# Probability split of a macaron attention layer: the low half moved ahead on VectorE, the high half moved between two exponentials on ScalarE

## The reference

```python
x = x + 0.5 * ffn(layernorm(x))
x = x + attn(layernorm(x), Wq, Wk, Wv, Wo, head_scale)
x = x + 0.5 * ffn(layernorm(x))
# attn: 16 heads of 128 over 4 key/value heads, rotary on q and k, causal
scores = einsum('bhid,bhjd->bhij', q, k) / sqrt(128)
attn = softmax(where(causal, scores, lowest))
out = einsum('bhij,bhjd->bhid', attn, v) * head_scale @ Wo
# ffn: ternary weights, hidden = silu(x wu) * (x wg), then wd
```

## Time and profile before

| | |
|---|---|
| median of 3 runs | 1085.21 us (1085.12 to 1085.38) |
| the profiled execution's own time | 1085.6 us |
| its span | 1083.8 us |
| busy, share of the span | PE 99%, DVE 85%, ACT 75%, POOL 66% |
| TensorE clock granted | 1.00 throughout |
| attention | about 187 to 909 us of the span |

### The profile page before, as it was taken

How to read it: one execution, slowest core, us unless ns; L and a number is a source line. 1 busy time by engine, 2 the same in 40 slices (tenths; PEclk the granted TensorE clock), 3 DMA queues, 4 the chain that set the end, 5 groups by cost and what they waited for, 6 DMA issues and landing times.

```text
span 1083.8 us, 26934 instructions
## 1 busy us (share of the span) xinstructions
PE 1068.4 (99%) x8537; PEld 845.5 (78%) x8537; DVE 921.7 (85%) x2313; ACT 815.3 (75%) x2040; POOL 713.0 (66%) x906
## 2 busy tenths in 40 slices
PE   8999999999999999999999999999999999999998
PEld 6556566788888888888888888888888887565665
DVE  6787886989999999999999999999999996433333
ACT  7887996887778787787877878778788785444443
POOL 3567675776777677777777777777777674444443
PEclk9999999999999999999999999999999999999999
DMA  9623222334434433343343433434334343100101
GB/s 346 169 40 59 52 47 39 52 74 87 74 72 82 80 73 76 71 82 75 73 81 71 82 70 73 82 73 82 71 69 82 73 82 70 30 19 19 39 19 39
DMA packets 262167, 79.94 MB, mean 74 GB/s; under 512 B 249329, under 2 KB 260849, under 8 KB 261873
## 3 DMA queue, kind: packets, MB, share of 16 engines
q1 hardware_dynamic: 261696, 79.19, 35.4%
q10 hardware_dynamic: 432, 0.27, 0.1%
HBM read 12.85 MB, written 4.19 MB: 16 GB/s over the span
## 4 chain that ended last, share of the span: by engine, by line
PE 73%; issue 10%; POOL 6%; ACT 5%; DVE 4%; DMA 1%; POOLq 0%; DVEq 0%; ACTq 0%; SPq 0%
PE bank L770 44%; PE bank L829 14%; POOL SCR L427 6%; PE bank L727 5%; PE bank L739 5%; PE bank L759 5%; ACT SCR L637 2%; DVE ARENA L1155 1%; ACT ARENA L644 1%; DVE SCR L973 1%; DVE bank L1179 1%; DMA SCR<-ARENA 0%; DVE X L963 0%; ACT SCR L515 0%; ACT ARENA L582 0%
## 5 line engine op out<-in xcount | busy, mean ns | idle before, releaser
L452 POOL TENSOR_SCALAR SCR<-SCR,RI 128x128 f32<-128x128 f32 (+1 forms) x512 | 309.5, 604 | 44.3 <-DVE RI L1151 4.2
L637 ACT ACTIVATE SCR<-bank,NM 128x128 f32<-128x128 f32 (+1 forms) x512 | 208.2, 419 | 123.4 <-DVE NM L1179 123.3
L417 POOL TENSOR_TENSOR SCR<-SCR 128x512 f32<-128x512 f32 x160 | 203.2, 1270 | 147.6 <-DVE SCR L973 146.1
L427 POOL TENSOR_TENSOR SCR<-SCR 128x512 f16<-128x512 f32 x128 | 151.0, 1182 | 161.2 <-ACT SCR L515 159.0
L829 PE MATMUL bank<-SCR 128*128 128x128 f32 (+1 forms) x1024 | 193.7, 332 | 4.1 <-ACT SCR L637 3.0
L534 ACT COPY SCR<-bank 64x512 f32<-64x512 f32 x320 | 185.5, 580 | 14.1 <-PE bank L770 8.2
L992 DVE SCALAR_TENSOR_TENSOR SCR<-SCR,CS,bank 128x512 f32<-128x512 f32 x128 | 95.1, 743 | 113.3 <-PE bank L739 100.2
L1155 DVE TENSOR_TENSOR ARENA<-SCR,ARENA 128x768 f16<-128x768 f32 x128 | 187.1, 1462 | 4.5 <-ACT ARENA L644 3.9
L770 PE MATMUL bank<-WOH,ARENA 128*128 128x256 f16 x1024 | 188.3, 273 | 0.8 <-DVE X L1188 0.8
L1179 DVE CUSTOM_DVE_ANT_0 bank<-bank,MASK,SCQ 128x128 f32<-128x128 f32 (+1 forms) x512 | 183.1, 417 | 3.5 <-PE bank L829 2.7
L545 ACT ACTIVATE SCR<-bank,SU 128x512 f32<-128x512 f32 x128 | 87.6, 685 | 106.4 <-PE bank L727 104.8
(11 more groups left out here) (120 smaller groups left out, 1653.1 us busy)
## 6 DMA issues: line engine op xcount, KB each, us to landing
out<-X SPq DMA_DIRECT2D x7, 512.0 KB, 2.9
X<-in_x SPq DMA_DIRECT2D x1, 2560.0 KB, 10.8
ARENA<-in_wq SPq DMA_DIRECT2D x1, 2048.0 KB, 13.8
ARENA<-in_wo SPq DMA_DIRECT2D x1, 2048.0 KB, 18.8
SCR<-ARENA SPq DMA_TRANSPOSE x128, 3.6
X<-in_x SPq DMA_DIRECT2D x3, 512.0 KB, 9.9
X<-in_wu SPq DMA_DIRECT2D x2, 512.0 KB, 5.8
X<-in_wg SPq DMA_DIRECT2D x2, 512.0 KB, 7.4
```

Of the source, the lines that this page charges most:

```text
L417: gp.tensor_tensor(dst, M1[:, m, :], M2[:, m, :], ALU.add).then_inc(add, 1)
L427: gp.tensor_tensor(HL[layer][:, f % 4, :], H32[layer][:, f % 2, :], HH[layer][:, f % 4, :], ALU.subtract).then_inc(s["hl_done"], 1)
L452: last = gp.tensor_scalar(EX[:, par, lo:hi], EX[:, par, lo:hi], RI[:, par, c:c + 1], PS, ALU.mult, ALU.mult)
L637: last = act.activation(EX[:, par, 384 * hh + lo:384 * hh + hi], SBK[hh][:, lo:hi], ACT.Exp, bias=NM[:, par, c:c + 1], scale=-1.0, accum_o ...
```

## The change

On ACT the high half of pair t-3 is made between the exponentials of the first and of the second head of pair t-2, no longer behind both. On DVE the low half of pair t-3 is made straight behind the rotation, ahead of the low half of the result and of the reciprocals. This holds in all steps; the operations are the same.

```diff
 act, in batch(b)
                             last.then_inc(ex, 1)
-                    if real(b, i, 3):
-                        e, par = t - 3, (i - 3) % 2
-                        act.wait_ge(pn, e + 1)
-                        wait(act, pt_t[par], 16 * (4 * b + (i - 3) // 2))
-                        act.copy(PR[:, par, 0:768], EX[:, par, :]).then_inc(p_hi, 1)
+                            if hh == 0 and real(b, i, 3):
+                                high_half(b, i)
+                    if real(b, i, 3) and not real(b, i, 2):
+                        high_half(b, i)
...
+            def high_half(b, i):
+                e, par = PAIRS * b + i - 3, (i - 3) % 2
+                act.wait_ge(pn, e + 1)
+                wait(act, pt_t[par], 16 * (4 * b + (i - 3) // 2))
+                act.copy(PR[:, par, 0:768], EX[:, par, :]).then_inc(p_hi, 1)
 ve, in batch(b), behind rope_mul(r, m, PJ[m]) and residual(0, TILES - 1)
+                    if real(b, i, 3):
+                        ve.wait_ge(p_hi, t - 2)
+                        par = (i - 3) % 2
+                        ve.tensor_tensor(PR[:, par, 768:1536], EX[:, par, :], PR[:, par, 0:768], ALU.subtract).then_inc(p_lo, 1)
                     if real(b, i, 6):
...
                         ve.reciprocal(RI[:, par, :], RS[:, par, :]).then_inc(rcp, 1)
-                    if real(b, i, 3):
-                        ve.wait_ge(p_hi, t - 2)
-                        par = (i - 3) % 2
-                        ve.tensor_tensor(PR[:, par, 768:1536], EX[:, par, :], PR[:, par, 0:768], ALU.subtract).then_inc(p_lo, 1)
```

## The result

The changed kernel takes **1107.64 us** (median of 4 runs, 1107.57 to 1109.19); the kernel before, run beside it, 1085.3 us. The ratio is 1.021, with a 95% interval of 1.0197 to 1.0221: 22 us slower. The profiled span is 1107.4 us against 1083.8; the execution profiled is the slowest of the four, 1109.19 us and so 1.55 above their median.

The account below looks back on a forecast made before the run. PE bounds the kernel, with DVE longer by a hair (0.33 us a sequence). Steps summed to 47.45 against 44.95 us, +2.5 over 15 sequences, +37.5: 1123, or 1122.7 against the median; range 1098 to 1138.

Parts of the forecast that it names:

- forecast as written: Whole kernel: the summed steps add 2.5 us a sequence, 1116 to 1130 us, chance 0.45.
- The closed loop: Reciprocals, multiplications, cast, subtraction, low half of the result, next reciprocals: claimed to close into a loop of one step.
- Early and late steps: Early: subtraction ahead of POOL's addition, reciprocals done at M + 4.17; late: behind the addition's start, M + 5.49; before, 4.72.
- Addition held: Early steps: DVE's subtraction holds POOL's addition to near M + 4.61; if not held, 44.9 to 45 a sequence, no change.
- step 2: Sequence step with the centring as extra: forecast late by a hair (0.03 us), 0.68 + 5.49 = 6.2 us.
- Centring ... I take 0.68: Step 2's DVE extra priced at 0.68 us, not 0.94, as if no longer partly held by POOL's multiplications.
- M: Start of DVE's maxima in a plain step, from which the forecast counts its times.
- one edge falls the other way: Rival: step 2 early at 4.85, step 3 still late; 46.6 a sequence, 1110 us; range 1095 to 1115, chance 0.25.
- Step 3: Step with the rows' low half (0.60) as extra: it holds the multiplications, late by 0.05, 6.1 us.
- 15 sequences: The count the 2.5 us was multiplied by, leaving out the first sequence's early steps: +37.5 us.
- PE's next scores of that head need them only at M + 5 or later: Second head's exponentials on ACT, 0.7 to 1.2 later: claimed hidden from PE, otherwise under 0.3 a step.
- What would show it: Expected profile signs, 500 to 600 us: PE about 94, DVE 5 to 8 idle, two subtraction lengths, reciprocals 5.5 apart.

Follow-up runs that it names:

- the loop cut short: The changed kernel without the second of POOL's four multiplications in each step: 1080.01 us, ratio to before 0.9929 to 0.9960.

## Why the prediction was right, and where it was off

The side was right, and the time lies in the range; the size was 15 us too large: +22.3 against the 37.5 forecast. Of the 1.22 us a sequence that were too much, 1.03 lie in one step. There is luck in it: the time lies outside the forecast as written (1116 to 1130, chance 0.45) and in a rival's span (1095 to 1115, 0.25), which the range took in, and the step that decided between the two was won by 0.02 us.

| step | forecast, us | measured, us |
|---|---|---|
| 0 | 6.8 | 6.75 |
| 1 | 5.25 | 5.16 |
| 2 | 6.2 | 5.17 |
| 3 | 6.1 | 6.41 |
| 4 | 6.2 | 6.03 |
| 5 | 5.85 | 5.73 |
| 6, 7 | 5.54 each | 5.49 each |
| sum | 47.45 | 46.23 |

(The forecast's terms as rounded here make 47.48. Measured from reciprocals to reciprocals, from 499.85 to 546.08.)

- **What bounds the kernel**: right. DVE and PE were level, and what the loop added to DVE's time showed in the whole.
- **The closed loop**: right, and shown from both sides: DVE's move alone makes every step late, and one multiplication less makes every step early.
- **Early and late steps**: right in kind and size. The late step was worked out as 5.49 and takes 5.49. The early step was worked out as 4.17; from the maxima to what follows the reciprocals it takes 4.11 in steps 0 and 1 and 4.25 in steps 2 and 4, so it saves 0.61 or 0.47 and not 0.55 each time.
- **"Addition held"**: right, 1.92 to 2.07 us against 1.27. This was the bound that no row showed. It costs no more in the early step itself, but it makes the next one late unless DVE has extras enough there: 0.92 us were enough in step 2, and 1.0 in step 3 were not.
- **The failed step: "Centring ... I take 0.68"**. With the change it takes 0.92 us of DVE (511.85 to 512.77), nearly the 0.94 of the earlier trace rows. The prediction reckoned that the multiplications, now behind the centring's start, would no longer hold it, and that much is so: they begin at 512.47. But it left out the addition, which by its own working, held by the subtraction, runs on to M + 4.61. It ran from 510.46 to 512.38, over the start of the centring at 511.85, and the first of the centring's two parts took 0.68 us and the second 0.40. Behind the last sequence no addition stands there, and the first part takes 0.38, both 0.77 as listed, about 0.7 of DVE:

```profile
926.45 0.77 DVE L1209 TENSOR_SCALAR SCR<-X,MV,RSTD 128x256 f32<-128x256 f32 x2
```

  The kernel with the addition behind the subtraction has the same pair beside a whole addition (332.56 and 332.27), and there it takes 1.45. So 0.68 was the right price for a centring that nobody holds, and the held addition made it 0.92; this is read from what overlaps in the traces, no run was made for it. With 0.24 more DVE work ahead of it, the cast was there 0.02 us ahead of the addition's start, and step 2 became early: 5.17 and not 6.2. That is the rival "one edge falls the other way", which gave 46.6 a sequence and 1110 us; it had the length, 0.94, but no reason for it.
- **Step 3** was late as forecast, by 0.14 and not 0.05 (cast at M + 1.98 against M + 1.84), since the held addition, 2.07 us, pushed the multiplications back. And the low half of the rows cost 0.99 us and not 0.60: 0.16 of waiting for its high half on ACT, which the rival had named at 0.3, and 0.83 for the operation itself beside the multiplications.
- **"15 sequences"**: 19.2 us of the 23.6 in span. I left the first sequence and the three steps behind the last out of the sum; they cost 2.0, in part perhaps by the lower clock of that execution, and 2.4.
- **"PE's next scores of that head need them only at M + 5 or later"**: wrong. With ACT's move in steps 4, 5 and 6 PE was there at M + 3.3 in step 4, in the changed kernel PE waits for the second head in DVE's step 5, till M + 4.8 (534.22), and DVE's reciprocals need the exponentials sooner still. The bound I gave, under 0.3 a step, held: ACT's move alone costs 0.55 a sequence. What it adds inside the full change isn't separated. With both moves in steps 0, 1, 2 and 4 it adds nothing, since PE never waits there, and with the loop cut short it adds nothing in any step.
- **"What would show it"**: DVE idle 5.3 in 100 us, reciprocals 5.5 apart, casts waiting for POOL, long additions in early steps: all there. PE's busy share was 98.4 and not 94: a sequence is 1.6 us, 3.5%, longer than PE's own work, and only 0.8 of it is listed as idle. The rest is in instructions that are held up after they began, which count as busy, as the scores at 533.30 (1.84 us for 1.48) show. The forecast of 94 had taken all waiting for idle time.

## What to carry to other kernels

Before an instruction is moved ahead of another on a full engine, follow what the second one releases, around all engines and back to the first: if the ring closes in one step, its whole length, handovers included, has to fit into that step. And what an instruction holds up on the way can hold up a third one, as the addition did to the centring. The same move can gain where an engine has other work to cover the ring's slack and lose where it has none, so in an unrolled program it is decided step by step: here four of eight steps, left out behind the last sequence, gave 0.57% and all eight cost 2.1%. And an order that is won by hundredths of a us is a fork, whose two arms both belong in the range.

## What the runs showed of the hardware

- The subtraction, which reads two operands in SBUF, and POOL's addition hold each other by who begins first, at a grain of hundredths: 0.02 us ahead, the subtraction takes 0.96 and the addition 2.07; 0.14 behind, the subtraction takes 1.95 and the addition 1.27.
- The centring, which has one large operand in SBUF, is held by the addition too: 0.77 us for its two parts with no addition beside it, 1.00 where the addition ran on for 0.53 us behind its start, 1.45 beside a whole one.
- The same hold reaches the rotation's second half: 0.76 to 0.79 us with the multiplications beside it, 0.82 beside an addition (527.15), 0.68 without; and POOL's multiplication under it took 0.90 (the chain above).
- The handover from reciprocals to multiplications is 0.33 us from the reciprocals' start in the ring (540.59 to 540.92), where the earlier trace rows gave 0.27.
